# Attention scores from two float32r parts on two row halves of the array, in place of three bfloat16 parts on 116 rows

## What is computed

```
for l in 0..3:                                # 16 heads of 16 channels
    q = norm(x) @ Wq[l] + bq[l];  k = ctx @ Wk[l] + bk[l];  v = ctx @ Wv[l] + bv[l]
    s = q @ k.T / 4                           # per head: 256 queries x 4096 keys
    layers 0, 1: s masked by mask[query, key];  layer 2: masked by key;  layer 3: no mask
    p = softmax(s);  layer 0 only: p = p * factor[query, key]
    x = x + (p @ v) @ Wo[l] + bo[l]
    x = x + self_part(l, norm(x));  x = x + feed_forward(l, norm(x))
```

## Time and profile before

| | |
|---|---|
| runs (3) | 1510.62, 1498.33, 1506.51 us; median 1506.51 |
| profiled execution | span 1502.7 us from the first to the last instruction; no separate time is shown for it |
| granted TensorE clock | 0.965 of full speed, mean |
| busy | PE 1371.0 us (91%), PEld 810.9 (54%), DVE 1010.4 (67%), ACT 857.6 (57%), POOL 567.3 (38%) |
| stages, about | projection 0 to 255; cross-attentions 255 to 531 (layer 0), 604 to 848 (layer 1), 950 to 1165 (layer 2), 1253 to 1463 (layer 3); the other parts between and after |

### The profile page before, as it was taken

One profiled execution on the slowest core, in us unless ns is written; L12 is line 12 of the kernel. 1 busy time (PEld: TensorE's weight loads), 2 busy tenths in 40 slices (PEclk: granted clock), 3 DMA queues, 4 the chain that ended last, 5 costly groups with the idle time before them and its releaser, 6 DMA issues. The chain is left out here.

```text
span 1502.7 us, 28955 instructions
## 1 busy us (share of the span) xinstructions
PE 1371.0 (91%) x10502; PEld 810.9 (54%) x10576; DVE 1010.4 (67%) x2314; ACT 857.6 (57%) x1308; POOL 567.3 (38%) x686
## 2 busy tenths in 40 slices
PE   8999797999999888699999888699999896999987
PEld 3766655455555456255555555255555582555555
DVE  4445486999999724778787053588884236888832
ACT  5143141899999621288888551167777211777762
POOL 4564252689989800655555340111110001111100
PEclk9999999799999978799999999899999998999999
DMA  8878998255456062266655195247776801667800
GB/s 265 280 255 256 245 258 274 33 77 83 65 82 146 2 89 39 53 96 90 88 81 143 59 185 202 75 71 109 104 113 190 118 9 45 96 96 108 156 2 8
DMA packets 126008, 178.30 MB, mean 119 GB/s; under 512 B 14733, under 2 KB 106021, under 8 KB 116646
## 3 DMA queue, kind: packets, MB, share of 16 engines
q1 hardware_dynamic: 111898, 161.04, 52.1%
...
...
## 5 line engine op out<-in xcount | busy, mean ns | idle before, releaser
L1003 ACT ACTIVATE prob_a<-ps 128x1024 f32<-128x1024 f32 x464 | 456.6, 1020 | 142.7 <-PE ps L835 95.4
L818 PE MATMUL ps<-kop,qop 116*128 116x512 bf16 x1024 | 344.9, 401 | 37.4 <-DMA qop<-qparts 22.9
L1027 DVE TENSOR_REDUCE best_a<-ps 128x1 f32<-128x512 f32 (+1 forms) x488 | 318.5, 709 | 48.9 <-PE ps L818 48.4
L835 PE MATMUL ps<-qop,kop 116*128 116x256 bf16 x2048 | 333.9, 274 | 7.1 <-ACT prob_a L1003 2.6
L835 PEld LDWEIGHTS ps<-qop,kop 116*128 116x128 bf16 x2048 | 193.8, 98 | 123.2 <-ACT prob_a L1003 20.7
L1023 DVE CUSTOM_DVE_ANT_0 dump_a<-ps,neg_q 128x512 bf16<-128x512 f32 (+1 forms) x244 | 165.7, 715 | 43.5 <-PE ps L818 41.3
L862 PE MATMUL ps<-prob_a,vop_a 128*32 128x256 f32 x3072 | 191.7, 383 | 3.1 <-POOL prob_a L1167 2.2
L818 PEld LDWEIGHTS ps<-kop,qop 116*128 116x128 bf16 x1024 | 95.3, 103 | 162.4 <-issue 65.5
L1137 POOL TENSOR_TENSOR used_a<-prob_a,gT 128x1024 f32<-128x1024 f32 x64 | 153.2, 2396 | 23.6 <-DVE used_a L1040 17.0
L1116 POOL CAST mpart_a<-nmax_a 128x2 bf16<-128x2 f32 x64 | 26.4, 412 | 351.9 <-DVE nmax_a L1032 351.9
L1167 POOL TENSOR_TENSOR prob_a<-prob_a,neg_k 128x1024 f32<-128x1024 f32 x48 | 102.5, 2135 | 92.0 <-ACT prob_a L1001 86.4
...
## 6 DMA issues: line engine op xcount, KB each, us to landing
...
```

Of the source, the lines that this page charges most:

```text
L818: return pe.matmul(out, qop[0:R_ALL, h, t * P:(t + 1) * P], kop[0:R_ALL, h % UNROLL, j * CHUNK:(j + 1) * CHUNK], start=True, stop=True)
L835: ins = pe.matmul(st_bank(n)[:, j * NT:(j + 1) * NT], kop[0:R_ALL, h % UNROLL, k * P:(k + 1) * P], qop[0:R_ALL, h, :], start=(j % 2 == 0), ...
L1003: act.activation(prob[:, n % NP, :], st_bank(n), ACT.Exp).then_inc(S("exp_done"), 1)
L1027: dve.tensor_reduce(out, bank, AX.X, ALU.max).then_inc(sem, 1)
```

## The change

Keys and queries are split into two parts of type float32r: the high part rounded to that type, the low part the rest. Three pairs replace seven (k0q0, k0q1, k1q0): 48 rows, two for the maximum, one for the mask, 51 in all (`R_ALL`). Partitions 0 to 63 (`HROWS`) hold the first half of the keys, 64 to 127 the second; the queries stand on both. `kop` is half as long and of a type twice as wide. A chunk or a by-key tile now uses the 51 rows of one half. Chunks take the halves by turns (`chunk_keys`); a by-key group takes two tiles from each half (`key_tile`), in the order 0, 2, 1, 3, so that neighbours lie on different halves and in different banks; the mask products of a group come after all four of its tiles. The order strings, the ring, the banks and all other stages stay. Six transfers load a head's key rows. `qop` is memset in full, four heads by VectorE, twelve by GpSimd; the later heads' loads wait for the latter. The maximum is split in two steps by GpSimd and placed by two ScalarE instructions. In the projection stage ScalarE's `second` and GpSimd's `third` go; each store of a key unit is 512 KB in place of 384. Mask and factor are laid out on the host in the new order of keys. The scratch space for dynamic transfers is set to 2048 bytes.

```diff
+HALVES = 2
+HROWS = P // HALVES
+HKEYS = KEYS // HALVES
+R_MAX = 2 * HD
+R_MASK = R_MAX + 2
+R_LOW = R_MASK + 1
+R_ALL = R_LOW + HD
+K_PIECES = [(half, part, half * HROWS + row) for part, row in ((HIGH, 0), (HIGH, HD), (LOW, R_LOW)) for half in range(HALVES)]
+Q_PIECES = [(slice(0, 2 * HD), half * HROWS) for half in range(HALVES)] + \
+           [(slice(0, HD), half * HROWS + R_LOW) for half in range(HALVES)]
+GROUP_AT = [0, 2, 1, 3, 4, 6, 5, 7]
+half_rows = lambda half: slice(half * HROWS, half * HROWS + R_ALL)
+def key_tile(i):
+    g, j = i // GROUP, i % GROUP
+    return HKEYS // P * (j // 2) + 2 * GROUP_AT.index(g) + j % 2
+def chunk_keys(j):
+    n = NCHUNK // HALVES
+    return (j + j // n) % HALVES, j % n * CHUNK
...
@@ class Operands
-        self.kop = ctx.enter_context(c.nc.sbuf_tensor("kop", [P, UNROLL, KEYS], BF16))
+        self.kop = ctx.enter_context(c.nc.sbuf_tensor("kop", [P, UNROLL, HKEYS], F32R))
...
@@ class QueryParts (before: first_and_second and rest_and_third)
+    def high(self, act, S, banks):
...
+            act.activation(self.half(self.qp[:, HIGH, :], mt), c.ps[:, banks[mt], 0:NT], ACT.Identity,
                            bias=c.bq[:, self.l, mt:mt + 1]).then_inc(S("q_part0"), 1)
+    def low(self, dve, S, banks):
...
+            dve.scalar_tensor_tensor(out=self.half(self.qp[:, LOW, :], mt), in0=c.ps[:, banks[mt], 0:NT],
+                                     scalar=c.bq[:, self.l, mt:mt + 1],
+                                     in1=self.half(self.qp[:, HIGH, :], mt).bitcast(F32),
+                                     op0=ALU.add, op1=ALU.subtract).then_inc(S("q_part1"), 1)
...
+    def load_rest(self, sp, S):
+        sp.wait_ge(S("qop_rest_set"), 1)
+        self.c.ops.load_q(sp, self.c.ops.S("q_rest"), slice(UNROLL, H), Q_PIECES)
...
@@ def project_context
-        kp = sb("kp", [P, SLOTS, 3, CHUNK], BF16)
+        kp = sb("kp", [P, SLOTS, PARTS, CHUNK], F32R)
...
-                    sp.wait_ge(S("k_split"), u + 1)
+                    sp.wait_ge(S("k_low"), u + 1)
...
-                    pe.wait_ge(S("k_rest"), u - 3)
+                    pe.wait_ge(S("k_low"), u - 3)
...
-            def second(u):
-                act.wait_ge(S("k_rest"), u + 1)
-                act.activation(kp[:, u % SLOTS, 1, :], rest[:, u % RESTS, :], ACT.Copy).then_inc(S("k_second"), 1)
...
-                    if u >= RESTS:
-                        dve.wait_ge(S("k_split"), u - RESTS + 1)
...
-            def third(u):
-                pool.wait_ge(S("k_second"), u + 1)
-                pool.tensor_tensor(kp[:, u % SLOTS, 2, :], rest[:, u % RESTS, :], kp[:, u % SLOTS, 1, :], ALU.subtract)\
-                    .then_inc(S("k_split"), 1)
+            pool.memset(c.qop[:, UNROLL:H, :].bitcast(F32), 0.0).then_inc(S("qop_rest_set"), 1)
...
@@ def attend, tensor: by_queries, by_keys, turn_max
-            return pe.matmul(out, qop[0:R_ALL, h, t * P:(t + 1) * P],
-                             kop[0:R_ALL, h % UNROLL, j * CHUNK:(j + 1) * CHUNK], start=True, stop=True)
+            half, first = chunk_keys(j)
+            rows = half_rows(half)
+            return pe.matmul(out, qop[rows, h, t * P:(t + 1) * P], kop[rows, h % UNROLL, first:first + CHUNK],
+                             start=True, stop=True)
...
-            for j in range(GROUP):
-                k = g * GROUP + j
+            for j in (0, 2, 1, 3):
+                half, at = divmod(key_tile(g * GROUP + j) * P, HKEYS)
+                rows = half_rows(half)
                 added = by_query and g not in SHIELD and g not in own
-                ins = pe.matmul(st_bank(n)[:, j * NT:(j + 1) * NT], kop[0:R_ALL, h % UNROLL, k * P:(k + 1) * P],
-                                qop[0:R_ALL, h, :], start=(j % 2 == 0), stop=(not added and j % 2 == 1))
-                if added and j % 2 == 1:
-                    ins = pe.matmul(st_bank(n)[:, (j - 1) * NT:(j + 1) * NT], c.identb[:, :],
-                                    c.neg_k[:, k - 1:k + 1, :], start=False, stop=True)
+                ins = pe.matmul(st_bank(n)[:, j * NT:(j + 1) * NT], kop[rows, h % UNROLL, at:at + P], qop[rows, h, :],
+                                start=(j % 2 == 0), stop=(not added and j % 2 == 1))
+            if added:
+                for j in (0, 2):
+                    k = g * GROUP + j
+                    ins = pe.matmul(st_bank(n)[:, j * NT:(j + 2) * NT], c.identb[:, :], c.neg_k[:, k:k + 2, :],
+                                    start=False, stop=True)
...
-                ins = pe.matmul(turn_out[0:R_MASK, t * P:(t + 1) * P], mpart[:, h % 2, t, :], c.identb[:, :],
+                ins = pe.matmul(turn_out[:, t * P:(t + 1) * P], mpart[:, h % 2, t, :], c.identr[:, :],
                                 start=True, stop=True)
...
@@ def attend, scalar: place_max
-            act.activation(qop[R_MAX:R_MASK, h, :], turn_out[R_MAX:R_MASK, :], ACT.Copy).then_inc(S("max_set"), 1)
+            for half in range(HALVES):
+                rows = slice(half * HROWS + R_MAX, half * HROWS + R_MASK)
+                act.activation(qop[rows, h, :], turn_out[rows, :], ACT.Copy).then_inc(S("max_set"), 1)
...
@@ def attend, gpsimd: split
-            step(pool.tensor_copy(part(0), nmax[:, h % 2, :]))
-            step(pool.tensor_tensor(mrest[:, h % 2, :], nmax[:, h % 2, :], part(0), ALU.subtract))
-            step(pool.tensor_copy(part(1), mrest[:, h % 2, :]))
-            pool.tensor_tensor(part(2), mrest[:, h % 2, :], part(1), ALU.subtract).then_inc(S("max_split"), 1)
+            pool.tensor_copy(both[:, :, :, R_MAX], found).then_inc(S("max_high"), 1)
+            pool.wait_ge(S("max_high"), h + 1)
+            pool.tensor_tensor(both[:, :, :, R_MAX + 1], found, both[:, :, :, R_MAX].bitcast(F32), ALU.subtract)\
+                .then_inc(S("max_split"), 1)
...
@@ def kernel
-    nc = bacc.Bacc("TRN2", target_bir_lowering=False, num_devices=1)
+    nc = bacc.Bacc("TRN2", target_bir_lowering=False, num_devices=1, dynamic_dma_scratch_size=2048)
```

165 lines of the change are left out of this document (77 added, 88 removed).

## The result

The changed kernel takes 1548.2 us (median of four runs, 1542.7 to 1558.1) against 1506.1: 2.9% slower, ratio 1.029 with a 95% interval of 1.024 to 1.034. The forecast was 1480 and faster; 1548 lies in the stated range, but on the slower side. The profiled execution took 1542.7 us with a span of 1541.4, 38.7 above the span before; it is the fastest of the four, and the two slowest, 1552.5 and 1558.1, had a lower mean granted clock (0.930 and 0.928, against 0.938).

What follows compares the result with a forecast made beforehand. TensorE was taken to bound layers 1 to 3, VectorE layer 0. Span 1502.7 - 13 (layer 1) - 13 (layers 2, 3) - 2 (tails) - 2 (query) + 3 (projection) = 1475.7; against the median 1480 us, range 1445 to 1560.

Steps and rivals of the forecast that it cites:

- Overlap of the halves: Score products on opposite row halves overlap: a by-key group falls from 0.43 to 0.26 us, saving 1.4 a head.
- rival 2: Cross stages: the halves don't overlap, only excursions and turns remain, +52 us, near 1558; 7%.
- TensorE's need in layers 2 and 3: TensorE's work per head there falls from 11.65 to 9.95 us, costs of added form changes and turned maxima included.
- Score products: A float32r product costs what a bfloat16 one does, 0.22 us for 512 columns; serial 197 ns loads were not assumed.
- Rival 3: Score products: float32r streams, or loads, like one float32 instruction; streams +164 us, about 1670, loads the same size; 7%.
- What becomes of it, layer 1: Layer 1's period becomes TensorE's need, 12.65 us, above ScalarE's 12.0; saves 13 us.
- Ring: Layers 2 and 3: three banks can't cover the double value block, path 2.59 us; 0.45 a head saved, 13 in all.
- Layer 0: Layer 0's cross-attention: VectorE's 15.57 us a head is the bound and stays untouched, so change 0.
- Query stage: Layers 1 to 3: 0.7 us a layer saved, 2 in all; memsets hidden, otherwise up to 3 us a layer.
- rival 1: Cross stages: the clock falls; mean 0.9 just loses the gain, near 1504, 0.8 gives about 1595; 15%.
- Projection: Projection stage: larger stores cost up to +7 us, a shorter chain wins some back; taken as +3.
- the end: Tails of the four layers, where no chunks remain: 2 us saved in all.

Runs made afterwards that it cites:

- experiment 1: Bench of TensorE alone, score products in six forms on constant operands: plain head 9.78 us in float32r, 8.89 in bfloat16, 11.61 as before.
- experiment 7: Changed kernel with score products reading constant bfloat16 tiles in place of the float32r operands: 1505.3 us.
- experiment 10: Kernel before, with ScalarE placing a head's maxima by two operations in place of one: layer 0 15.98 us for 15.86, layer 1 13.77 for 13.59.
- experiment 13: Changed kernel with late GpSimd fill, repeated chunk pairs, start fills; then stand-ins and later values; evener order; layer 1's order too: 1543.0, 1524.9, 1513.4, 1517.0 us.
- Experiments 8: Changed kernel, layers 2 and 3 reordered: values spread 1590.7 us, chunk between the two value blocks 1567.6, last block moved into the next head 1537.4.
- experiment 6: Changed kernel with GpSimd's zero fill of the query operands waiting until VectorE has finished the norm: 1544.9 us.
- experiment 11: Changed kernel with the old ScalarE copy and GpSimd subtraction put back behind the projection's key parts, stores waiting for both: 1573.1 us.

## Why the prediction was wrong, by its steps

**Overlap of the halves: right.** By-key groups take 0.24 (forecast 0.26); rival 2 is out.

**TensorE's need in layers 2 and 3: 9.78 for a forecast of 9.95, by luck.** Two errors cancel. The format, put at nothing, costs 0.89 a head in experiment 1. And a term was left out: I let chunks overlap only where two stand side by side, but a lone chunk overlaps the by-key group next to it, 0.11 each, some 0.9 a head for eight lone chunks. In bfloat16 the need is 8.89.

**Score products: the step that failed first.** I took the lower end for a float32r product and let the eight overlapping loads of the earlier trace rows excuse the 197 ns load. Alone that is nearly so: 2.04 for 16 chunks. In pairs between other forms a float32r pair costs 0.11 more, and in the kernel the format is worth 0.74 a head in layers 2 and 3 and 0.64 in layer 1 (experiment 7). With bfloat16 the period there is 11.19, the forecast's 11.2. Rival 3 had the cause in the format, but at 2.5 a head and more. Whether load or stream makes the difference was not separated.

**What becomes of it, layer 1: wrong.** I let the period be TensorE's need, 12.65. The need is 13.31 (12.07 in bfloat16) and the period 13.94. Of the 0.63 above the need, the second placement costs 0.18 in the kernel before (experiment 10); the rest is open. A wait behind the double blocks, as in layers 2 and 3, would be a guess: experiment 13 took those blocks apart in layer 1, and the period grew.

**Ring: right in kind, too small.** The path past the double block is 0.42 + 1.87 + 0.53 = 2.82, not 2.59. I let VectorE keep 0.88 of its 1.32 us of idle time a head. It kept all of it: 1.48 are left (11.93 less 10.45 busy). Experiments 8 and 13 show that the place of the blocks set the period: 11.33 and 11.08 without the double block.

**Layer 0: 0 forecast, 0.44 a head measured.** VectorE's work was not changed, but its durations were, as GpSimd's weighting came to lie beside one more of its own. I had excluded that cost without bounding it. My 15.68 was also one period among several; their mean before is 15.86.

**Query stage: the failed claim was named.** "If they don't, the price is up to 3 us a layer": 2.69 measured. The fill was to run beside the norm. It did, but VectorE's norm step doesn't run beside it.

**Clock: rival 1, in part.** It had 15%, for steady heads at a mean below 0.9. It came at the starts (14.4 us longer, of which experiment 13's best version keeps 5) and, in some executions, in steady heads. My argument against it, values in all columns, held for the steady heads of the changed kernel's profiled execution, but not for seven heads of layer 3 in experiment 6, values and all; the starts have none, and I looked at no start. In the earlier trace rows TensorE was busy at 0.50, which was the hint that busy time isn't enough.

**Projection: -9.3 where I took +3.** Both terms were named. The shorter chain brings more than the larger stores cost; neither was measured by itself (experiment 11).

**In sum**, 38.7 us were added where 27 were to go, a difference of 66: steady heads 44 (+17.6 for -26), starts 14, between the layers 17 (+15.0 for -2; the norm beside the fills is 8 of it, the rest wasn't tested), the end 3 (+1.0 for -2), less 12 in the projection. Of the 44, over the 13 periods counted, the format is 28 (0.74 x 13 in two layers, 0.64 x 13 in one), layer 1 beyond the format 8, layer 0 6, and the rest is that the forecast counted 14.5 periods.
